# Two attentions' softmax divided on token rows behind the values' products, and images embedded four abreast

## The reference

```python
patches = lax.conv_general_dilated(pixel_values, conv_w, window_strides=(PATCH, PATCH), padding='VALID', ...)
...
h = jnp.concatenate([h, _L0_txt_ref(x_txt, L0_txt_token_embeddings)], axis=1)
...
attn_prob = jax.nn.softmax(content_score + pos_score, axis=-1)
attn_vec = jnp.einsum('bnij,bjnd->bind', attn_prob, v).reshape(b, s, D_MODEL)
attn_out = attn_vec @ Wo + bo
...
attn = jax.nn.softmax(scores, axis=-1)
out = jnp.einsum('bhqk,bkhd->bqhd', attn, v)
...
x = x + a @ attn_proj_w + attn_proj_b
```

## Time and profile before

| what | us |
|---|---|
| median of 3 runs (1941.24 to 1943.97) | 1941.75 |
| the profiled execution, its own time | 1940.76 |
| its span (the work recorded on the engines) | 1938.6 |
| from the start to the first group of the first attention | 62.76 |
| first attention, from there to the slot experts' dispatch | 328 |
| a middle group of it | 78.07 |
| second attention, 783.70 to 970.00 | 186 |
| a middle group of it | 46.13 |

### The profile page before, as it was taken

One profiled execution on the slowest core, in us unless ns is written; L12 is line 12 of the kernel. 1 busy time (PEld: TensorE's weight loads), 2 busy tenths in 40 slices (PEclk: granted clock), 3 DMA queues, 4 the chain that ended last, 5 costly groups with the idle time before them and its releaser, 6 DMA issues.

```text
span 1938.6 us, 30939 instructions
## 1 busy us (share of the span) xinstructions
PE 1574.3 (81%) x10048; PEld 1105.6 (57%) x10048; DVE 748.0 (39%) x2156; ACT 655.0 (34%) x1667; POOL 384.6 (20%) x451
## 2 busy tenths in 40 slices
PE   7877777747778778788888599589899999689993
PEld 4554554533323335555567488556666776578883
DVE  1254544562111146655533512154643424531112
ACT  0456465511000023566642011134444432103331
POOL 5121111210000012322200145311211100023331
PEclk9679888755776768899998589889999999659997
DMA  7133141352999740000003345400000200135553
GB/s 195 31 94 85 39 123 40 83 199 69 354 312 308 227 128 1 1 1 0 0 1 79 89 149 177 108 1 1 0 0 0 98 0 1 47 93 154 156 139 88
DMA packets 92810, 177.79 MB, mean 92 GB/s; under 512 B 35306, under 2 KB 53904, under 8 KB 90680
## 3 DMA queue, kind: packets, MB, share of 16 engines
q1 hardware_dynamic: 78528, 129.86, 23.3%
q10 hardware_dynamic: 7056, 30.67, 4.8%
q0 software_dynamic: 7136, 16.10, 2.8%
HBM read 149.61 MB, written 26.99 MB: 91 GB/s over the span
## 4 chain that ended last, share of the span: by engine, by line
PE 45%; issue 24%; DVE 13%; DMA 10%; ACT 4%; POOL 2%; SPq 2%; DVEq 0%; POOLq 0%; ACTq 0%
PE bank L1595 9%; DMA WM<-in_fc 6%; PE bank L2044 6%; PE bank L2032 5%; PE bank L2034 4%; PE bank L1685 2%; PE bank L1786 2%; DVE MXU L877 2%; PE bank L1697 2%; DVE SMU L883 2%; PE bank L1714 2%; PE bank L1724 2%; PE bank L1778 1%; PE bank L2000 1%; DMA WM<-rows_out 1%
## 5 line engine op out<-in xcount | busy, mean ns | idle before, releaser
L1595 PE MATMUL bank<-XT,AREA 96*128 96x408 f32 (+1 forms) x640 | 239.6, 533 | 33.0 <-ACT XT L1371 15.7
L1595 PEld LDWEIGHTS bank<-XT,AREA 96*128 96x128 f32 (+1 forms) x640 | 122.0, 196 | 139.6 <-issue 100.4
L1685 PE MATMUL bank<-KZ,QT 128*102 128x102 f32 x1152 | 150.0, 273 | 7.0 <-ACT PB L1415 3.6
L1685 PEld LDWEIGHTS bank<-KZ,QT 128*102 128x102 f32 x1152 | 131.3, 186 | 22.3 <-issue 11.8
L632 POOL TENSOR_TENSOR RS<-VE,expo 102x4 f32<-102x4 f32 (+1 forms) x53 | 53.1, 1001 | 451.4 <-DVE VE L822 392.6
L646 POOL TENSOR_TENSOR PB<-PB,RCU 102x306 f32<-102x306 f32 x96 | 66.9, 697 | 371.1 <-DVE RCU L884 371.1
L2044 PE MATMUL bank<-WM,KZ 128*128 x660 | 120.7, 331 | 0.0
L2032 PE MATMUL bank<-KZ,SLOTS 128*128 128x128 f32 x660 | 116.4, 301 | 2.5 <-issue 2.5
L1697 PE MATMUL bank<-AREA,OT 128*102 128x192 f32 x384 | 89.3, 346 | 31.8 <-DVE SLOTS L1112 11.2
L1714 PE MATMUL bank<-PT,V 102*32 102x102 f32 (+1 forms) x1152 | 88.1, 276 | 28.4 <-DVE OT L898 28.4
L2044 PEld LDWEIGHTS bank<-WM,KZ 128*128 128x128 f32 x660 | 108.3, 194 | 0.4
(11 more groups left out here) (308 smaller groups left out, 2767.7 us busy)
## 6 DMA issues: line engine op xcount, KB each, us to landing
AREA<-in_fc SPq DMA_DIRECT2D x10, 1536.0 KB, 21.1
SLOTS<-in_m3w SPq DMA_DIRECT2D x33, 384.0 KB
WM<-in_fc ACTq DMA_DIRECT2D x5, 2304.0 KB, 18.8
WM<-in_fc SPq DMA_DIRECT2D x6, 1536.0 KB
AREA<-in_fc ACTq DMA_DIRECT2D x4, 2304.0 KB, 20.8
SLOTS<-in_m1w SPq DMA_DIRECT2D x33, 256.0 KB
AREA<-pos_scratch SPq DMA_DIRECT2D x16, 459.0 KB
pos_scratch<-AREA SPq DMA_DIRECT2D x8, 913.5 KB
```

What stands on the lines that cost most here:

```text
L1595: last = pe.matmul(dst, lhsT, rhs, start=n == 0, stop=n == len(pieces) - 1)
L1685: last = pe.matmul(psum[k][0:T, cols(j)], QT[:, tile, cols(bb)], KALL[:, unit % per_tile * (HEADS // per_tile) + tile, cols(bb)], start=Tr ...
```

## The change

In the first two attentions the exponentials are no longer divided before the values' product. DVE's sums and reciprocals for each unit and POOL's multiplication go. V gets a 17th column of ones. The values' product swaps its operands: a head's turned exponentials PT are stationary (102 columns), its 17 value columns move, and the result has tokens in rows, with the sum of the exponentials in the 17th column. For each image DVE takes one reciprocal over 12 heads and one multiplication over 192 elements (`normed`), PE turns the result with two transposes, DVE copies it, and PE projects with two products over 96 rows, for which Wo and proj1 are loaded in 12 pieces each. PE turns a unit as soon as ACT has its exponentials, and in the first attention it overwrites a scores bank as soon as DVE has read it. The third attention keeps its form, but DVE's copy to OT stands ahead of the minimum of its step.

The start changes too. Four images share a bank, in rows 0, 32, 64 and 96, and their products alternate. H is cleared by DVE. V's clearing goes. Eight of the gathers stand ahead of the first powers, and eight behind KZ's clearing; DVE waits for the first four before group 0 and for the other twelve before it prepares group 1. The slots are loaded before the first weights and normalised behind all images.

```diff
-        STEPS = UNITS + 7
+        STEPS = UNITS + 9
+        NORMED, TURNED, PROJECTED = UPB + 5, UPB + 6, UPB + 8
...
+        OR = [OT[j][0:T, 3:5, :].rearrange("p k t -> p (k t)")[:, 0:D] for j in range(2)]
...
+            def load_heads(dst, src, name):
+
+                for h in range(HEADS):
+                    r, to = 32 * (h % 4), 16 * (h % 6)
+                    load(dst[to:to + 16, h // 6, :], src[r:r + 16, h // 4, :], name)
+
+            load_heads(wo0, t["Wo"], "wo0_loaded")
...
-            pool.memset(H[:], 0.0).then_inc(sem["constants_ready"], 1)
...
+            words(0, GB, "words_loaded")
+            words(GB, NB // 2, "words_behind")
...
+            pool.wait_ge(sem["halves_cleared"], at.now("halves_cleared"))
+            words(NB // 2, NB, "words_behind")
...
             with at.loop(pool, NG - 1):
-                powers(1)
-                probabilities()
-                powers(1)
+                powers(2)
             dispatch_powers()
-            probabilities()
             powers(1)
...
+            def normed(bb, pos):
+
+                dve.wait_ge(sem["values_ready"], at.take("values_ready"))
+                o = psum[VALUES[pos][bb % len(VALUES[pos])]][0:T, 0:17 * HEADS].rearrange("p (h d) -> p h d", d=17)
+                rc = RCU[:].rearrange("p a b -> p (a b)")[:, 0:HEADS]
+                step(dve.reciprocal(rc, o[:, :, 16]))
+                give(tt(OR[bb % 2].rearrange("p (h d) -> p h d", d=16), o[:, :, 0:16], wide(rc, 16), ALU.mult),
+                     "values_taken")
+
+            def attention_rows(pos, finish):
+                for s in range(STEPS + 1):
+                    if batch_at(s, NORMED) is not None:
+                        normed(batch_at(s, NORMED), pos)
+                    if batch_at(s, TURNED + 1) is not None:
+                        src = full(PROJBANK)[0:KD, 0:2 * T].rearrange("p (k t) -> p k t", k=2)
+                        free(dve.tensor_copy(OT[batch_at(s, TURNED + 1) % 2][0:KD, 0:2, :], src), PROJBANK)
+                    if s < UNITS:
+                        minima(s, pos)
+                    if batch_at(s, PROJECTED + 1) is not None:
+                        finish(batch_at(s, PROJECTED + 1), full(PROJBANK)[0:T, 0:D], PROJBANK)
+                at.one("exp_ready", UNITS)
...
+            dve.memset(H[:], 0.0).then_inc(sem["rows_cleared"], 1)
+            step(dve.memset(by_head(16)[:, :, 16:17], 1.0))
+            dve.wait_ge(sem["rows_cleared"], 1)
             dve.wait_ge(sem["patches_loaded"], 64)
             dve.wait_ge(sem["constants_ready"], 1)
             step(tt(posE[:, 0, :], posE[:, 0, :], posE[:, 1, :], ALU.add))
-            for first in range(0, NB, 2):
-                if first == 10:
-                    unit_slots()
+            for g in range(NG):
                 k = at.bank(OBANKS)
-                o = full(k)[0:NPATCH, 0:2 * D].rearrange("p (b d) -> p b d", b=2)
-                for j in range(2):
-                    last = tt(H[0:NPATCH, first + j, :], o[:, j, :], posE[:, 0, :], ALU.add)
+                o = full(k)
+                for j in range(GB):
+                    last = tt(H[0:NPATCH, g * GB + j, :], o[32 * j:32 * j + NPATCH, 0:D], posE[:, 0, :], ALU.add)
                 free(last, k)
+            unit_slots()
...
+                if isinstance(g, int):
+                    dve.wait_ge(sem["words_loaded"], 16 * GB)
+                else:
+                    dve.wait_ge(sem["words_behind"], 16 * (NB - GB))
...
-                            pe.wait_ge(sem["exp_ready"], at.take("exp_ready"))
+                    elif pos:
+                        pe.wait_ge(sem["probs_in"], mins + n - len(banks) + 1)
+                    else:
+                        pe.wait_ge(sem["exp_ready"], exps + n - len(banks) + 1)
...
+                def projection_of_rows(s):
+
+                    bb = batch_at(s, TURNED)
+                    if bb is not None:
+                        taken(bb)
+                        k, p = claim(None, PROJBANK)
+                        for m in range(2):
+                            last = pe.transpose(p[0:KD, cols(m)], OR[bb % 2][:, m * KD:(m + 1) * KD], ident[0:T, 0:T])
+                        rows_moved[bb] = filled(last, PROJBANK)
+                    bb = batch_at(s, PROJECTED)
+                    if bb is not None:
+                        moved(rows_moved[bb])
+                        k, p = claim(None, PROJBANK)
+                        for m in range(2):
+                            last = pe.matmul(p[0:T, 0:D], OT[bb % 2][0:KD, m, :], wo[:, m, :], start=m == 0, stop=m == 1)
+                        filled(last, PROJBANK)
+
+                def value_products(n):
+
...
+                        if dv == 16:
+                            last = pe.matmul(psum[k][0:T, 17 * h:17 * h + 17], PT[n % 2][:, j, :],
+                                             by_head(dv)[:, bb * HEADS + h, 0:17], start=True, stop=True)
+                            continue
...
-                            last = pe.matmul(psum[k][row:row + rows, cols(tile)],
-                                             by_head(dv)[:, bb * HEADS + h, :], PT[n % 2][:, j, :],
-                                             start=True, stop=True)
...
-                        pe.wait_ge(sem["probs_ready"], at.take("probs_ready"))
+                        if dv == 16:
+                            pe.wait_ge(sem["exp_ready"], exps + n + 1)
+                        else:
+                            pe.wait_ge(sem["probs_ready"], at.take("probs_ready"))
...
-            for first in range(0, NB, 2):
+            for g in range(NG):
                 k, p = claim(OBANKS)
-                for j in range(2):
-                    last = product(p[0:NPATCH, j * D:(j + 1) * D],
-                                   [(patchT[:, n, first + j, :], convT[:, n, :]) for n in range(KP // 128)])
+                for n in range(KP // 128):
+                    for j in range(GB):
+                        last = pe.matmul(p[32 * j:32 * j + NPATCH, 0:D], patchT[:, n, g * GB + j, :], convT[:, n, :],
+                                         start=n == 0, stop=n == KP // 128 - 1)
```

163 lines of the change are left out of this document (86 added, 77 removed).

## The result

The changed kernel takes 1956.23 us (median of 5 runs, 1952.56 to 1961.3), the kernel before 1941.82 beside it: a ratio of 1.0098, 95% interval 1.0073 to 1.0123.  The change makes the kernel 1% slower. The forecast was 1884 us, its range 1864 to 1915: the sign was wrong.

A forecast was written before the change was run, and what follows sets the result against it. The prediction took chains, not a full engine, to bound each stage. Gains of 24 (start), 7 (second attention), 24 (first) and 2 (third) sum to 57 us off 1940.76: 1883.8, said as 1884 us, range 1864 to 1915.

The forecast's parts named there:

- The start: Before the first group's loop: embedding in strips ends sooner; gain 24 us, after 4 off for DVE's unexplained 11.98 us idle.
- The full step: One unit of PE's scores, values and transposes in the attentions: 0.63 + 0.57 + 0.31 = 1.51 us, PE becoming the bound.
- both bounding rows: Profile rows pricing a values' record of the full step: 0.091 us (102 loaded, 8 moved) and 0.103 us (scores' weight load).
- The second attention's work: Second attention, one group's stretch: 29.2 us instead of 31.2; gain 7 us in four groups, bounds 3 and 9.
- The first attention: First attention, after the wait for image 1's positions: 30.8 us instead of 38.7 per group; gain 24 us for four groups.
- the one us taken off: First attention: 1 us less gain per group, as it was open whether the low clock is left as soon as before.
- The rival that came true: Attentions: low clock takes over, slower than before, chance 0.10; narrower form, first attention low from its wait on, 1960 us.
- The row named for it: Evidence for the low-clock rival: PE works 13.20 us without a gap, 66 columns moving to 128 loaded, clock staying 0.50.
- the argument against it: Against the low-clock rival: half of a step stays scores and transposes, under which the second attention holds 1.00.
- The third attention: Third attention: copy to OT ahead of the minimum saves PE's waits of 3.3 us; gain 2 us, bounds -2 and 3.3.
- Code loading: Rival at the branch into the loop: DVE's 11.98 us idle comes again, start gains 13 to 16; 1892 to 1896, chance 0.12.
- strips: Rival in the start: embedding products in different strips don't run abreast, start gains 5 us; total 1903 us, chance 0.05.

The follow-up runs named there:

- early17: Changed kernel (17 columns moved) with PE's waits in the first two attentions filled with extra products and image 3's position rows one step earlier: 0.9533 of the kernel before.
- warm_early: Changed kernel with 42 moved columns in the values' product, PE's waits in the first two attentions filled, image 3's position rows one step earlier: 0.9507 of the kernel before.
- filler_wait: Changed kernel with four extra products of 300 moving columns before PE's wait for image 1's positions in each first-attention group: 0.9953 of the kernel before.
- warm17: Changed kernel (17 columns moved) with extra products of 200 moving columns in PE's waits in the first two attentions: 0.9612 of the kernel before.
- start_only: Kernel before with only the start's changes, all attentions as before: 0.9824 of the kernel before.

## Why the prediction was wrong, step by step

**The start held.** PE's embedding and DVE's normalisation, for the earlier trace rows:

```profile
9.38 10.73 PE L1818 MATMUL bank<-KZ 128*25 128x192 f32 x192 [9.38 <-DMA ON<-in_conv_b]
```
```profile
26.79 5.04 DVE L843 TENSOR_SCALAR XN<-H,MV,RS 102x192 f32<-102x192 f32 x4 [1.15 <-POOL RS L643]
```

PE ends at 20.1 (21.3 said), 10.73 us for the 12 said and 0.056 us a record; the slots' normalising took 21.73 to 23.72, the 2.0 said; the loop's first values begin at 35.27 (34.6 said). DVE's 11.98 us without a releaser did not come back in this run; yet over the kernels with the new start the first turning lies between 31.0 and 38.9 us, so an open size of some us was right. The first turning came 28.3 us earlier, for the 24 said with 4 taken off.

**The full step was mis-sized, on the safe side.** In the second attention at clock 1.00, for the earlier trace rows:

```profile
887.08 0.70 PE L1731 MATMUL bank<-KZ,QT 128*102 128x102 f32 x6
...
887.53 0.62 PEld L1781 LDWEIGHTS bank<-V,PT 102*102 102x102 f32 x6
887.62 0.63 PE L1781 MATMUL bank<-V,PT 102*102 102x17 f32 x6
...
888.10 0.45 PE L1804 MATMUL bank<-ident,ON 102*102 102x102 f32 x3
...
888.39 0.52 PE L1731 MATMUL bank<-KZ,QT 128*102 128x102 f32 x4
```

From values to transposes 0.48 us, not 0.57, and a step of 1.31, not 1.51: both bounding rows were too dear. The loads do take 0.62 us for six, but the first lie under the scores' last columns and the last under the next product, so less than their sum stands in the step. The price of the Trainium skill, "TensorE: Matmul & The Clock Gate", section "LDWEIGHTS (loading the stationary operand)", is 85 ns a load, by an estimate from it 0.51 us for six, and was nearer than either row.

**The second attention's work was right, its clock not.** From the first scores at 881.54 to the last projection's end at 909.06 are 27.5 us, 29.2 said, 31.2 before. But the clock fell at the end of every group (to 0.90 and 0.87 in the middle ones), and groups took 45.8 to 47.7 us instead of 44: gain 0.4, not 7. With the ends filled a group is 42.48.

**The first attention is the step that failed.** It was to gain 24 us and took 53.7 more, at a mean clock of 0.55 in a middle group; a clock under 0.85 there was named as a sign of being wrong. Its work and waits were about right: with the clock mostly held, groups are 71 to 73 us in early17 and 69 to 73 in warm_early, for the 71 said, though in both image 3's position rows come a step earlier. One wait was far off, image 3's positions at 0.4 us for PE, 3.18 measured in filler_wait; in the changed kernel's middle groups the slower PE hides it. The error that decided is the sentence "the first 7.8 us are the same work at the low clock, which holds 0.50 until 277.4", and the one us taken off for the doubt behind it. It took the point at which the clock comes back from the old trace, though the values' products with 102 moved columns, which stood in those steps, are what the change takes out. (From 270.10 to 277.4 are 7.3 us, not 7.8.) And "up to 270.10 nothing moves" left out that the projections then run low too. Their price stood in the trace of before, whose first group entered the loop at 0.50. The first scores of the first and of the third group there:

```profile
99.04 1.36 PE L1685 MATMUL bank<-KZ,QT 128*102 128x102 f32 x6
```
```profile
256.48 0.78 PE L1685 MATMUL bank<-KZ,QT 128*102 128x102 f32 x6
```

From the loop's first product (62.76 and 230.72) that is 36.3 us at the low clock and 25.8 at the high one: 10.5 us a group. The changed kernel's third group takes 36.3 us too (222.69 to 258.98). So the sum of the low time was too small: at 0.83 before, (1 - 0.83) / 0.5 of 326.5 are 111 us at 1.2 GHz; at 0.57 after, 327 of 380.2. That the low clock is the loss, warm17 shows, in which the changed kernel with its waits filled takes 0.961 of the time before; why the clock does not come back in the 17-column steps stays open.

**The rival that came true** is the first, in its narrower form: the first attention low from its wait on, 1960 us said, 1956 measured. It had 0.10. That the numbers meet is in part luck: the rival, too, left out the projections at the low clock, so a middle group took 96.1 us, where 71 and 19 make 90, while the start and the third attention gained 4 and 7 us more than the sum had for them. The row named for it, 13.20 us without a gap at 0.50, was worth more than the argument against it, that the second attention holds 1.00: holding and coming back are two things. The page of the Trainium skill (section "What's actually happening"), by which the clock falls after idleness and sustained activity lifts it again, agrees with the falls looked at here, filler_wait's above all. With the missing return it does not agree: three stretches of the changed kernel in which PE is busy 10.00 of 10.00 us stayed at 0.50, and the measurement decides:

```profile
274.50:284.50 10.00, 10.00 (x60) 9.15 (x58) 3.44 (x8) 5.58 (x18) 0.00 (x0) 0.50 0.58 149
284.50:294.50 10.00, 10.00 (x59) 9.89 (x59) 4.16 (x9) 4.61 (x15) 0.00 (x0) 0.50 0.23 50
294.50:304.50 10.00, 10.00 (x58) 9.89 (x59) 4.16 (x10) 4.12 (x13) 0.00 (x0) 0.50 0.00 0
```

**The third attention gained 9.2 us, not 2.** PE's waits for DVE's additions went from 8.2 to 5.8 us,

```profile
PE bank L1746 <- DVE H L1343: 5.8, 8, 1.1
```

the 3.3 for OT are gone, and a fall of the clock at 1431 us that the old trace had is gone with them (6.8 us at half clock, 3.4): 2.4 + 3.3 + 3.4 = 9.1. The bound of 3.3 had left the clock out here too. Code loading and strips, the other rivals, did not come.

## What to carry to other kernels

Where a change thins out PE's work (fewer columns moved for each column loaded), read not only whether the clock holds in such steps but what brings it back after each wait of PE, and whether that work is what the change removes; then price everything up to the next return at half clock. The waits themselves may be old and cheap: here the low clock behind them came to cost about 20 us a group (96 for 73 to 77 with the waits filled), half of that in projections that the change does not touch. Filling the 1.7 us wait alone gave back 6 of them (90 us). When PE has become the bound, dense products in its waits can pay (4 to 5% here); in the old form, where DVE paced the steps, they gave nothing that could be told in the kernel's time.

## What the hardware showed that was not expected

- PE can be busy without a gap for 30 us and stay at 1.2 GHz (274.50 to 304.50 of the changed kernel). With extra products of 500 moving columns in each step, 11.7 us a group at full clock, the clock was at 1.00 through the steps, and a middle group took 92.3 us for 95.8 and 96.1 in the changed kernel's two profiles.
- 17 or 42 moved columns behind 102 loaded ones cost the same to 0.04 us in a unit, at either clock.
- One wait of 1 to 3 us starts a fall in some places and none in others: the 1.23 us ahead of image 0's positions left start_only at 1.00 (to 287.52), and in warm17 the same wait, to 199.50, was followed by a fall at 200.75. Nothing here tells why.
